# New task orders on five engines in an attention and feed-forward kernel

## The reference

```python
q, k, v = x @ wq, x @ wk, x @ wv
q, k = rope(q) / 128 ** 0.5, rope(k) / 128 ** 0.5     # half of the width turns
p = softmax(q @ k.T - 1e30 * (i < j))
x = layernorm(x + (p @ v) @ wo)
h = gelu(x @ binarized(w1).T + b1, approximate=False)
x = layernorm(x + h @ binarized(w2).T + b2)
```

## Time and profile before

| what | value |
|---|---|
| median of three runs | 276.79 us (276.37 to 276.82) |
| span of the profiled execution | 274.5 us |
| TensorE (PE) covered by matmuls | 260.9 us, 95% |
| VectorE (DVE) | 229.6 us, 84% |
| ScalarE (ACT) | 224.7 us, 82% |
| GpSimd (POOL) | 167.2 us, 61% |
| chain that ended last | TensorE 81%, VectorE 6%, ScalarE 5%, issue 3%, DMA 2% |

### The profile page before, as it was taken

One profiled execution on the slowest core, in us unless ns is written; L12 is line 12 of the kernel. 1 busy time (PEld: TensorE's weight loads), 2 busy tenths in 40 slices (PEclk: granted clock), 3 DMA queues, 4 the chain that ended last, 5 costly groups with the idle time before them and its releaser, 6 DMA issues.

```text
span 274.5 us, 5184 instructions
## 1 busy us (share of the span) xinstructions
PE 260.9 (95%) x1485; PEld 208.7 (76%) x1487; DVE 229.6 (84%) x638; ACT 224.7 (82%) x398; POOL 167.2 (61%) x258
## 2 busy tenths in 40 slices
PE   7899999999999999999999999999999999999960
PEld 3678989987779588868879688868886878897630
DVE  2799999999999996999979987998689738537984
ACT  3378964565897989996998999898999799999972
POOL 3033132613625698399821998497819887887772
PEclk9999999999999999999999999999999999999997
DMA  7944596479657936833685318825830720200323
GB/s 178 166 61 87 107 145 98 115 163 192 104 132 160 199 94 153 180 47 78 173 187 127 82 39 249 184 71 151 189 73 27 197 55 2 76 2 0 111 90 108
DMA packets 58012, 31.94 MB, mean 116 GB/s; under 512 B 33408, under 2 KB 54400, under 8 KB 57984
## 3 DMA queue, kind: packets, MB, share of 16 engines
q1 hardware_dynamic: 57024, 30.76, 50.4%
q10 hardware_dynamic: 960, 0.85, 1.3%
HBM read 9.18 MB, written 4.19 MB: 49 GB/s over the span
## 4 chain that ended last, share of the span: by engine, by line
PE 81%; DVE 6%; ACT 5%; issue 3%; DMA 2%; ACTq 1%; POOL 0%; POOLq 0%
PE pair L589 18%; PE bank L606 18%; PE bank L632 5%; PE bank L674 4%; PE pair L650 4%; PE pair L651 4%; PE bank L620 4%; PE bank L682 4%; PE bank L683 4%; PE bank L719 2%; DMA sin_sb<-in_sin_dram 2%; PE pair L663 2%; PE pair L665 2%; PE pair L664 2%; PE bank L639 2%
## 5 line engine op out<-in xcount | busy, mean ns | idle before, releaser
L391 POOL TENSOR_TENSOR hid_lo<-hid,hid_hi 128x1024 fp32r<-128x1024 f32 x28 | 66.0, 2386 | 19.7 <-ACT hid_hi L1075 19.7
L1004 ACT ACTIVATE prob<-pair,negmax 128x128 f32<-128x128 f32 (+3 forms) x64 | 47.2, 742 | 14.2 <-DVE negmax L1457 12.5
L606 PE MATMUL bank<-probT,xa 128*128 128x512 f32 (+3 forms) x160 | 54.2, 482 | 0.0
L1457 DVE CUSTOM_DVE_ANT_0 pair<-pair,mask_row 128x128 f32<-128x128 f32 (+3 forms) x64 | 47.9, 759 | 6.1 <-PE pair L589 5.5
L606 PEld LDWEIGHTS bank<-probT,xa 128*128 128x128 f32 x160 | 29.1, 190 | 20.2 <-issue 15.3
L341 POOL TENSOR_TENSOR xT_lo<-xT,xT_hi 128x512 fp32r<-128x512 f32 x14 | 18.0, 1288 | 40.4 <-ACT xT_hi L1034 40.4
L1467 DVE STREAM_TRANSPOSE turned<-prob 128x128 f32<-128x128 f32 (+7 forms) x56 | 39.5, 724 | 0.5 <-ACT prob L1004 0.5
L589 PE MATMUL pair<-qkT_hi 128*128 128x512 f32 (+3 forms) x96 | 36.0, 375 | 0.8 <-DVE qkT_lo L1619 0.3
L1068 ACT ACTIVATE hid<-pair,b_sb,alpha 128x1024 f32<-128x1024 f32 x28 | 32.9, 1209 | 0.1
L589 PE MATMUL pair<-qkT_lo,qkT_hi 128*128 128x512 f32 (+3 forms) x96 | 32.8, 342 | 0.0
L589 PE MATMUL pair<-qkT_hi,qkT_lo 128*128 128x512 f32 (+3 forms) x96 | 32.8, 342 | 0.0
(11 more groups left out here) (116 smaller groups left out, 649.9 us busy)
## 6 DMA issues: line engine op xcount, KB each, us to landing
probT<-turned SPq DMA_DIRECT2D x96, 116.0 KB, 2.3
probT<-turned SPq DMA_DIRECT2D x128, 52.0 KB, 2.0
xq<-in_L_attn_x_dram SPq DMA_DIRECT2D x28, 128.0 KB, 4.0
xa<-in_L_attn_x_dram SPq DMA_DIRECT2D x7, 512.0 KB, 4.7
out_dram<-res SPq DMA_DIRECT2D x7, 512.0 KB, 3.3
hid<-in_L_ffn_w_dram SPq DMA_DIRECT2D x2, 256.0 KB, 3.2
out_dram<-res SPq DMA_DIRECT2D x2, 256.0 KB, 2.3
xa<-in_L_attn_x_dram SPq DMA_DIRECT2D x1, 256.0 KB, 3.6
```

The costliest lines, as they stand in the source:

```text
L391: pool.tensor_tensor(hid_lo[:, j, :], hid[:, j, :], hid_hi[:, j, :].bitcast(F32), ALU.subtract).then_inc(s_hid_lo[j], 1)
L606: ins = pe.matmul(bank_of["px", g, c][:, 0:n * P], xa[c % 2][:, j, :], probT[g][:, :, TG * j:TG * j + n, :].rearrange("p n m i -> p m n i" ...
L1004: act.activation(prob[r % 3][:, 0:(r + 1) * P], pair_of["score", r, c][:, slice(*columns(r))], ACT.Exp, scale=-1.0, bias=negmax[:, r:r + 1 ...
L1457: dve.tensor_tensor_reduce(mine, mine, mask_row[:, T - (r + 1) * P:T], -1.0, -MASKED, ALU.add, ALU.min, negmax[:, r:r + 1]).then_inc(s_max ...
```

## The change

The tasks of all five engines stand in new orders. The set of tasks is the same on SyncE, VectorE, ScalarE and GpSimd, and on TensorE but for the passes over zeros. Nothing in a task is changed, but `fill` can now be called before three double banks have been in use. The last stretch of every list is as before: the last 42 calls of TensorE, the last 9 of ScalarE, 14 of VectorE, 29 of GpSimd and 12 of SyncE.

The passes over zeros in the opening were `keep_warm(4)` ahead of the first projection, `keep_warm(3)` ahead of the first turn, `keep_warm(6)` behind the second turn and `fill(2)` ahead of the third turn; they become `fill(4)`, `fill(5)` and `fill(6)` in the first three places, and none in the fourth. The eight at the start and the nine in the closing stay.

The diff, cut to the opening, the first carry and the closing:

```diff
 # SyncE
             stripes(2)
             carry(0, 0)
+            tokens(1)
             stripes(3)
-            tokens(1)
+            carry(0, 1)
             stripes(B - 4)
-            carry(0, 1)
             carry(1, 1)
+            carry(0, 2)
             tokens(2)
             stripes(B - 3)
-            carry(0, 2)
             carry(1, 2)
...
 # TensorE
             def fill(n):
 
-                wait_freed(*list(pair_of)[-len(pairs)])
+                if len(pair_of) >= len(pairs):
+                    wait_freed(*list(pair_of)[-len(pairs)])
...
             turn_x0(0)
             turn_x0(1)
-            keep_warm(4)
+            fill(4)
             project(0, 0)
             project(1, 0)
-            keep_warm(3)
+            fill(5)
             turn_qk(0, 0)
             turn_qk(1, 0)
-            keep_warm(6)
+            fill(6)
             setup_turn_wv()
             scores(0, 0)
             scores(1, 0)
-            fill(2)
+            scores(2, 0)
+            setup_wvo()
             turn_qk(2, 0)
-            scores(2, 0)
             scores(3, 0)
-            setup_wvo()
+            turn_qk(3, 0)
             project(0, 1)
-            turn_qk(3, 0)
             project(1, 1)
+            scores(4, 0)
             setup_turn_sgn1()
             setup_turn_sgn2()
-            scores(4, 0)
...
-            weigh_group(0, 0, 3, 0)
             scores(3, 1)
             scores(4, 1)
+            weigh_group(0, 0, 3, 0)
...
             project_out(0, B - 2)
+            weigh_group(1, 0, 3, B - 2)
+            weigh_group(1, 4, 7, B - 2)
             scores(4, B - 1)
-            weigh_group(1, 0, 3, B - 2)
             scores(5, B - 1)
-            weigh_group(1, 4, 7, B - 2)
-            turn_row(4, B - 1)
+            scores(6, B - 1)
             turn_x1(0, B - 3)
             turn_x1(1, B - 3)
-            scores(6, B - 1)
             scores(7, B - 1)
+            turn_row(4, B - 1)
+            down(0, B - 4)
+            project_out(1, B - 2)
             up(0, B - 3)
-            project_out(1, B - 2)
-            up(1, B - 3)
-            down(0, B - 4)
             down(1, B - 4)
...
 # ScalarE
             xT_high(0, 0)
             xT_high(1, 0)
+            xT_high(0, 1)
+            setup_signs()
             tok_copy(0, 0)
+            xT_high(1, 1)
             qkT_high(0, 0)
             qkT_high(1, 0)
             tok_copy(1, 0)
-            xT_high(0, 1)
-            setup_signs()
             exponentials(0, 0)
             exponentials(1, 0)
-            xT_high(1, 1)
             exponentials(2, 0)
...
+            exponentials(6, B - 1)
+            second_norm(0, 3)
+            second_norm(1, 3)
+            second_norm(2, 3)
+            exponentials(7, B - 1)
+            y_half(0, B - 4)
             row_copy(4, B - 1)
...
             pxT_copy(0, B - 1)
+            x1T_high(0, B - 2)
             hidden_high(2, B - 3)
-            x1T_high(0, B - 2)
+            x1T_high(1, B - 2)
             row_copy(5, B - 1)
             row_copy(6, B - 1)
-            x1T_high(1, B - 2)
...
 # VectorE
             x0T_low(0)
             x0T_low(1)
+            x_squares(0, 1)
+            x_squares(1, 1)
             rotate(0, 0)
             first_rotation_sum(0)
             rotate(1, 0)
-            x_squares(0, 1)
             qkT_low(0, 0)
             qkT_low(1, 0)
             first_rotation_sum(1)
             setup_wvT()
             row_max(0, 0)
             row_max(1, 0)
-            x_squares(1, 1)
+            row_max(2, 0)
+            setup_wvo()
             turn_row(0, 0)
-            row_max(2, 0)
+            turn_row(1, 0)
             row_max(3, 0)
-            setup_wvo()
-            turn_row(1, 0)
             turn_row(2, 0)
-            turn_row(3, 0)
             qkT_low(2, 0)
             qkT_low(3, 0)
             rotate(0, 1)
             rotate(1, 1)
             row_max(4, 0)
+            turn_row(3, 0)
             row_max(5, 0)
...
             hidden_low_half(0, 2, B - 1)
+            hidden_low_half(0, 3, B - 1)
             hidden_high_half(1, 1, B - 1)
-            hidden_low_half(0, 3, B - 1)
```

More of the change, by code:

```diff
@@ L1208, in _ @@
             xT_high(1, B - 3)
-            x1T_high(1, 1)
+            tok_copy(1, B - 4)
+            x1T_high(0, 1)
             exponentials(5, 3)
@@ L1212, in _ @@
             pxT_copy(1, 2)
+            x1T_high(1, 1)
             qkT_high(0, B - 4)
@@ L1664, in _ @@
             row_max(1, 1)
+            row_max(2, 1)
             qkT_low(2, 1)
@@ L1682, in _ @@
             residual1(3, 0)
+            row_max(7, 1)
+            turn_row(5, 1)
             statistics1(0, 0)
-            turn_row(5, 1)
-            row_max(6, 1)
-            row_max(7, 1)
-            reciprocals(0, 1)
+            qkT_low(0, 2)
+            statistics1(1, 0)
+            statistics1(2, 0)
             rotate(1, 2)
-            statistics1(1, 0)
+            statistics1(3, 0)
             turn_row(6, 1)
-            statistics1(2, 0)
-            statistics1(3, 0)
-            qkT_low(0, 2)
             turn_row(7, 1)
-            x_squares(0, B - 4)
-            x_squares(1, B - 4)
             qkT_low(1, 2)
+            first_norm(0, 0)
+            first_norm(1, 0)
             rotate(0, 3)
-            row_max(0, 2)
             residual1(4, 0)
@@ L1734, in _ @@
             first_norm(7, 0)
+            residual1(1, 1)
+            residual1(2, 1)
+            residual1(3, 1)
+            x1T_low(0, 0)
+            turn_row(4, 2)
+            row_max(6, 2)
+            row_max(7, 2)
+            rotate(1, 3)
+            x_squares(0, B - 4)
+            x1T_low(1, 0)
+            x_squares(1, B - 4)
+            turn_row(5, 2)
+            qkT_low(0, 3)
             statistics1(0, 1)
-            turn_row(4, 2)
-            row_max(7, 2)
-            x1T_low(1, 0)
-            turn_row(5, 2)
+            statistics1(1, 1)
             turn_row(6, 2)
-            reciprocals(0, 2)
-            statistics1(1, 1)
-            statistics1(2, 1)
-            statistics1(3, 1)
             turn_row(7, 2)
+            qkT_low(1, 3)
             residual1(4, 1)
@@ L1785, in _ @@
             row_max(5, 3)
+            rotate(1, B - 4)
+            first_norm(4, 1)
+            first_norm(5, 1)
+            first_norm(6, 1)
+            row_max(6, 3)
+            first_norm(7, 1)
+            x1T_low(0, 1)
             turn_row(4, 3)
-            row_max(6, 3)
+            turn_row(5, 3)
             x1T_low(1, 1)
-            turn_row(5, 3)
-            turn_row(6, 3)
             row_max(7, 3)
@@ L1793, in _ @@
             qkT_low(1, B - 4)
+            x_squares(0, B - 2)
             statistics1(0, 2)
-            statistics1(1, 2)
-            turn_row(7, 3)
-            statistics1(2, 2)
             residual1(4, 2)
@@ L1801, in _ @@
             residual1(7, 2)
+            turn_row(6, 3)
+            turn_row(7, 3)
+            qkT_low(2, B - 4)
+            rotate(0, B - 3)
+            statistics1(1, 2)
+            statistics1(2, 2)
             statistics1(3, 2)
+            residual2(0, 0)
             statistics1(4, 2)
@@ L1908, in _ @@
             qkT_low(1, B - 2)
+            turn_row(5, B - 3)
+            turn_row(6, B - 3)
+            reciprocals(0, B - 3)
             residual1(4, B - 4)
-            turn_row(7, B - 3)
             residual1(5, B - 4)
@@ L1913, in _ @@
             residual1(7, B - 4)
-            statistics2(1, 1)
+            x_squares(1, B - 1)
+            turn_row(7, B - 3)
             statistics1(4, B - 4)
@@ new lines, in _ @@
+            statistics1(5, B - 3)
+            qkT_low(2, B - 1)
+            statistics1(6, B - 3)
+            statistics1(7, B - 3)
+            row_max(0, B - 1)
+            row_max(1, B - 1)
+            row_max(2, B - 1)
+            qkT_low(3, B - 1)
+            row_max(3, B - 1)
+            residual1(0, B - 2)
+            turn_row(0, B - 1)
+            turn_row(1, B - 1)
+            statistics1(0, B - 2)
+            turn_row(2, B - 1)
+            statistics2(0, 3)
+            statistics2(1, 3)
@@ L1981, in _ @@
+            turn_row(3, B - 1)
+            residual1(1, B - 2)
+            residual1(2, B - 2)
+            residual1(3, B - 2)
             first_norm(4, B - 3)
+            statistics1(1, B - 2)
             first_norm(5, B - 3)
-            row_max(1, B - 1)
-            turn_row(0, B - 1)
-            qkT_low(2, B - 1)
-            qkT_low(3, B - 1)
             first_norm(6, B - 3)
             first_norm(7, B - 3)
-            residual1(0, B - 2)
-            statistics2(0, 3)
-            row_max(2, B - 1)
```

627 lines of the change are left out of this document (294 added, 333 removed).

## The result

The changed kernel takes 296.84 us (median of four runs, 295.68 to 297.76) against 276.78 (276.37 to 276.82) in the same comparison: a ratio of 1.072, with an interval of 1.068 to 1.075. It is slower, as forecast, but by 20 us in place of 2.4, far outside the range of 275.9 to 282.2.

What follows compares the result with a forecast made beforehand. The prediction took TensorE's own work to bound the long middle. Its terms, 1.7 + 1.4 + 0.6 + 0.4 - 0.4 - 1.3 = +2.4, on 276.8 gave 279.2 us, range 275.9 to 282.2.

Steps and rivals of the forecast that it cites:

- What bounds the kernel: From 22 to 217 us TensorE's own work binds; an order can change only the opening, waits and the closing.
- The rest of the middle, -0.4 (-0.8 to +1.5): Moved scores, turns, ups and weighings keep their work; new orders may remove half of TensorE's 0.8 us of waits.
- a credit of 1.0 us in the opening: Second rotation sum no longer runs beside GpSimd's xT_lo, so it shortens; 1.0 us taken off the opening's delay.
- The opening, +1.7 and +1.4 for the clock: Early transposes wait for strips and delay the first rotation, +1.7; idle TensorE falls to 1.2 GHz before first turn, +1.4.
- The first carry, +0.6: carry(0, 0) starts later, so TensorE's first weighing waits a little for its data; +0.6 us (0 to 1.5).
- SyncE's queue, +0.4: Later carries on SyncE, and stripes(5) behind carry(0, 2) landing near 85 us; +0.4 us (0 to 1.5).
- The closing, -1.3: Earlier x1T_highs, second_norms and a hidden_low_half swap remove TensorE's waits at the end; -1.3 us (-2.6 to +0.3).
- the turning of row 7: In the closing, named with ScalarE's own queue as late next, once the earlier waits go; within the -1.3 us.
- late transfers stop the engines repeatedly (283.1): Rival: late strips or carries stop VectorE and TensorE repeatedly between 40 and 95 us; 283.1 us, chance 0.11.

Runs made afterwards that it cites:

- after_accum: The changed kernel with first_norm also writing an accumulator that nobody reads, orders untouched; 281.87 us, ratio 1.018.
- before_accum: The kernel before the change with first_norm also writing an accumulator that nobody reads; 276.91 us, ratio 1.0005.
- before_closing_rows: The kernel before with three ScalarE moves: both x1T_highs of column 6 earlier and row_copy(7, 7) right behind row_copy(6, 7); 276.18 us, ratio 0.9992.
- before_norms_late: The kernel before with only three first_norms of column 2 moved behind row_max(4, 4), where GpSimd is busy; 282.64 us, ratio 1.020.
- before_squares_early: The kernel before with only x_squares(0, 1) and x_squares(1, 1) moved ahead of rotate(0, 0) on VectorE; 281.56 us, ratio 1.018.

## Why the prediction was wrong

- **What bounds the kernel.** That the middle is bound by TensorE's own work held for the kernel before. The conclusion that an order could then change only waits did not: it took each instruction's duration as its own, whatever runs beside it.
- **The rest of the middle, -0.4 (-0.8 to +1.5): the step that failed.** It measured +17.6 with the carries. 12.7 of that (216.82 - 204.17) goes with the form of first_norm, and the timed runs give 14.7 us for it, the clock's fall behind the stall included. Of the 4.5 us by which the middle of after_accum is still longer than that of before_accum (204.17 - 199.68), TensorE's waits make up 3.9, the largest 2.7 at scores(3, 3) behind the late strips and 1.0 at a weigh_row. The row that should have warned was in the prediction: the rotation sum of 1.78 us beside GpSimd, against 0.69 without. It was read as a credit of 1.0 us in the opening, not as a rule that all moved first_norms had to be held against. It is a row of another operation, though: no first_norm of the kernel before is held up by more than 0.1 us, so its trace could raise the suspicion and not settle it.
- **The rule behind it.** The Trainium skill (SBUF — State Buffer, Who interferes with whom) says that VectorE and GpSimd share one pair of ports as an exclusive lock, held for a whole instruction: of an operation of VectorE in a two-port mode (or with two inputs in SBUF, against one of GpSimd that reads SBUF) and an operation of GpSimd, the one that starts first goes to its end and the other waits; it names tensor_scalar among those that can enter such a mode, except in the form that writes its accumulator. The trace agrees in three points: 2.38 us until hidden_low ends, 0.403 us in the exempt form, and 1.78 against 0.68 for the sum with two inputs in SBUF. Beside GpSimd's operation on 128x4 numbers at 129.91 no such wait is seen, and there the measurement decides. That the lock is the mechanism is the Trainium skill's statement; the runs show that the form and the neighbour decide.
- **The opening, +1.7 and +1.4 for the clock: right, as far as one execution tells.** The rotation starts at 12.55 (12.8 forecast), the first turn at 14.66 (15.1), the second rotation sum takes 0.68, the clock is at 0.53 in the stretch from 14.6 to 18.2, and the first mark is 2.75 us late. after_accum, whose profiled execution kept its clock there, has 27.28 at that mark: 1.41 for the delay, 1.34 for the fall, each known to some 0.7 us only, by the scatter of the first marks above. The prediction cited the Trainium skill (TensorE: Matmul & The Clock Gate, Part 1: The HAM clock gate) for a change of level whose moment varies from run to run; the traces agree in that the same opening shows a fall and none, but the idle time differed too (3.75 us in the change, 3.32 in after_accum). At the end of the kernel the fall shows less: the executions of after_accum with the lower mean clock are 0.1 to 0.7 us longer, though no trace shows where in them it fell.
- **The first carry, +0.6: not there.** It landed at 39.25 and the first weighing started at 39.59, straight behind scores(4, 1): delay and moves cancel.
- **SyncE's queue, +0.4: not separated.** VectorE waits 1.09 us for the strips of column 5 at 87.09, and 2.63 in after_accum; with that wait gone there, the next ones take its place and the time shows no gain.
- **The closing, -1.3: right in kind, -0.94 in size** (-1.18 in after_accum). project_out(0, 7) and up(0, 6) follow at 250.96 and 251.83 without a hole. What the prediction named as late next, the turning of row 7, is what returns at up(2, 6) when the two x1T_highs are moved alone; of the kernels run, only those with the whole new order keep the gain. One reason is seen above: in before_closing_rows two first_norms collide with GpSimd.
- **The rivals.** That late transfers stop the engines repeatedly (283.1) describes the largest wait that is left in after_accum at 281.87, but not the main loss. No rival had VectorE's own instructions become longer.

## What to carry to other kernels

Before moving an operation of VectorE, look at what GpSimd does at its new place: where the profile has one row of an operation that takes much longer beside GpSimd than alone, suspect it of other operations too, and price a move by the length of the operation that it lands on. What VectorE loses reaches the end only where TensorE waits for it: 4.2 us cost 6.2 in the middle (before_norms_late), and 4.2 in the closing at most the 0.9 us of the two holes behind them (before_closing_rows). A mean duration that changes between two kernels with the same instructions is read first, ahead of all waits; and where such a collision can't be avoided by order, try the same operation in another form, which here gave back 14.7 of 20.1 us without moving anything.

## What the runs showed of the hardware that was not expected

- A tensor_scalar of 128x128 in f32 from SBUF to SBUF took 0.34 us alone and up to 2.49 us beside GpSimd's operations on 128x512 and 128x1024 numbers, always to the end of one of these; beside one on 128x4 numbers (1.04 us) it was not lengthened. With the accumulator written it took 0.40 us and 0.085 us to read that out, beside GpSimd or not. Transposes of VectorE from SBUF to SBUF and its statistics were not lengthened (693 against 695 ns for 128x512, 275 against 276; none of the change's statistics over 0.296 us).
- A stall of TensorE cost more than itself: behind 4.06 us without a matmul (the change, at 107.02), and behind two waits of 2.15 and 1.39 us (before_norms_late), the clock of the next stretch was 0.51 and 0.52. Ahead of the first turn it fell behind 3.75 us without a matmul (the change) and 4.07 (before_squares_early), and stayed full behind 3.32 (after_accum).
- The price of a fall in the opening was 3.0 us at the end of before_squares_early. In the change it was 1.34 us at the first mark, the difference of two single executions, and the executions of after_accum with a lower mean clock were 0.1 to 0.7 us longer at the end.
